# A transformer block with attention and a mixture of experts: the shared tiles leave PSUM by ScalarE, their sums move into the expert cycles, and all engines get a new order between the batches and the experts

## The reference

```python
h = layernorm(x) * (1 + ca) + sa                      # per batch
w = exp(tanh((h @ W + b) @ h.T * lw)); w = w * off_diag
x = x + ga * ((w / (sum(w) + 1e-7)) @ h)
h = layernorm(x) * (1 + cb) + sb
logits = h @ Wg                                       # 8 experts, the best 2 are taken
sparse = sum over the 2 chosen of softmax weight * (relu(h @ W1[e] + b1[e]) @ W2[e] + b2[e])
shared = relu(h @ Ws1 + bs1) @ Ws2 + bs2              # every token
out = x + gb * (sparse + shared)
```

## Time and profile before

| | |
|---|---|
| runs | 664.46, 659.73, 660.33 us; median 660.33 |
| profiled execution | span 665.5 us from the first to the last instruction; no time of its own is given beside the span |
| TensorE matmul busy | 618.6 us, 93% |
| VectorE busy | 457.9 us, 69% |
| ScalarE busy | 397.5 us, 60% |
| GpSimd busy | 343.3 us, 52% |
| mean granted TensorE clock | 0.982 |
| indirect DMAs on GpSimd | L576 x64 (of one source) 1008 ns each; L780 x138 1032 ns each |

### The profile page before, as it was taken

The page is one execution under the profiler, slowest core; times in us unless marked ns, Lnnn a source line. Parts: engine busy times, 40 slices in busy tenths (PEclk is TensorE's granted clock), DMA queues, the critical chain, the costliest instruction groups (busy, mean ns, idle before and its releaser), DMA issues.

```text
span 665.5 us, 13395 instructions
## 1 busy us (share of the span) xinstructions
PE 618.6 (93%) x4311; PEld 560.6 (84%) x4311; DVE 457.9 (69%) x1415; ACT 397.5 (60%) x635; POOL 343.3 (52%) x341
## 2 busy tenths in 40 slices
PE   3898999999999998977898999999999999999995
PEld 3587988898889886866798999998989898898995
DVE  7889797989898969766666564544444454452698
ACT  3587887877878756524346556565555646463541
POOL 4541706757575765657460465655565656465100
PEclk9899999999999999887999999999999999999998
DMA  8030000111111111111165466656666665521692
GB/s 299 27 158 1 1 1 17 37 34 33 34 33 38 33 42 33 37 39 43 49 196 200 129 197 190 181 172 193 195 188 182 187 182 178 175 65 30 268 386 113
DMA packets 29884, 76.44 MB, mean 115 GB/s; under 512 B 7126, under 2 KB 11374, under 8 KB 29712
## 3 DMA queue, kind: packets, MB, share of 16 engines
q1 hardware_dynamic: 20480, 58.49, 27.2%
q0 software_dynamic: 8640, 16.93, 7.5%
q10 hardware_dynamic: 720, 0.47, 0.2%
HBM read 53.53 MB, written 23.24 MB: 115 GB/s over the span
## 4 chain that ended last, share of the span: by engine, by line
PE 33%; DVE 8%; issue 5%; another core or an unknown queue 2%; DMA 2%; POOL 2%; ACT 1%; SPq 0%; POOLq 0%; ACTq 0%; DVEq 0%
PE value L1940 12%; PE score L1733 5%; PE misc L1940 5%; PE score L1731 5%; PE score L1732 4%; PE value L1991 2%; POOL rows_x L576 2%; DVE h_hi L1271 1%; DMA h_t<-rows_z 1%; ACT work L967 1%; DVE tile_y L1560 1%; PE misc L1772 1%; DVE tile_y L1552 0%; DMA lw<-rows_x 0%
## 5 line engine op out<-in xcount | busy, mean ns | idle before, releaser
L780 POOL DMA_INDIRECT rows_z<-tile_y,tags x138 | 142.5, 1032 | 118.8 <-issue 37.5
L1731 PE MATMUL score<-h_hi,h_lo 128*128 128x512 f32 (+1 forms) x252 | 94.9, 376 | 3.9 <-DVE rows_all L1177 3.8
L1759 PE MATMUL value<-w_ring,work 128*128 128x129 f32 x768 | 93.8, 279 | 1.6 <-ACT work L840 1.0
L1759 PEld LDWEIGHTS value<-w_ring,work 128*128 128x128 f32 x768 | 91.2, 194 | 4.1 <-issue 1.6
L967 ACT ACTIVATE work<-score,w_ring 128x512 f32<-128x512 f32 (+1 forms) x96 | 53.2, 616 | 61.7 <-PE score L1733 44.5
L1733 PE MATMUL score<-h_hi,h_lo 128*128 128x512 f32 (+1 forms) x252 | 89.4, 355 | 0.0
L1732 PE MATMUL score<-h_hi,h_lo 128*128 128x512 f32 (+1 forms) x252 | 88.9, 353 | 0.0
L576 POOL DMA_INDIRECT rows_x<-work,slot x64 | 64.5, 1008 | 45.5 <-issue 16.3
L838 ACT ACTIVATE work<-work 128x1024 f32<-128x1024 f32 x64 | 67.2, 1050 | 27.2 <-DVE work L1168 22.1
L1168 DVE TENSOR_TENSOR work<-score,lw 128x1024 f32<-128x1024 f32 x64 | 76.6, 1216 | 2.7 <-PE score L1733 1.2
L967 ACT ACTIVATE work<-score,w_shared 128x512 f32<-128x512 f32 x64 | 39.9, 685 | 57.9 <-PE score L1733 45.6
(11 more groups left out here) (254 smaller groups left out, 1269.0 us busy)
## 6 DMA issues: line engine op xcount, KB each, us to landing
w_ring<-packs SPq DMA_DIRECT2D x24, 578.0 KB
rows_all<-packs SPq DMA_DIRECT2D x23, 578.0 KB
lw<-rows_x SPq DMA_DIRECT2D x24, 260.0 KB
res<-x SPq DMA_DIRECT2D x8, 512.0 KB, 6.3
h_t<-rows_z SPq DMA_DIRECT2D x3, 1024.0 KB, 11.0
mod<-mod_rows SPq DMA_DIRECT2D x1, 2560.0 KB, 10.1
rows_z<-tile_y,tags POOLq DMA_INDIRECT x142
rows_all<-rows_z SPq DMA_DIRECT2D x2, 1024.0 KB, 13.0
```

The costliest lines, as they stand in the source:

```text
L780: nc.gpsimd.indirect_dma_start(rows_z[:, :], bass.IndirectOffsetOnAxis(ap=tags[pos][:, k, 0:1].bitcast(I32), axis=0), tile_y[par][:, k, :] ...
L1731: nc.tensor.matmul(out, a_lo, b_hi, start=True, stop=False)
L1759: ins = nc.tensor.matmul(value[:, s // 3, c0:c0 + D + 1], prob[:, t % 4, s * P:(s + 1) * P], normal[b % 3][:, t, :], start=(t == 0 and s % ...
```

## The change

- **ScalarE takes the front shared tiles out of PSUM.** A new `evacuate_shared(n)` waits for `down_ready` n + 1 and copies the bank, without bias or gate, into the place in `h2_t` that held the tokens of tile n, and signals `y_evac`. The eight copies stand between the relus of the front tiles, the last behind `expert_x(0, 0)`.
- **VectorE adds them later.** `shared(n)` is gone. `add_shared_part(b, part)` does bias, gate and sum for a whole batch of 1024 tokens, one instruction a call; twelve calls for batches 0 to 3 stand in the six steps of expert cycles 1 and 2. These two cycles are written out on VectorE, and its loop begins at cycle 3. A wait for all eight copies stands ahead of cycle 0.
- **TensorE's order.** `shared_up(0)` and `shared_up(1)` come before the wait for `attend(7)`; then down 0, up 2, down 1, both transposes of batch 7, up 3, gate logits, down 2, ranks, up 4, total ranks, down 3. From `shared_up(5)` on nothing changes. Before, the order was up 0, down 0, up 1, up 2, transposes, gate logits, down 1, ranks, down 2, up 3, total ranks, up 4, down 3.
- **VectorE's order.** Both first splits come before `attend(7)`; `take_ranks(6)` and `assign(6)` come before `scale_attended(7)`; `moments_2(7)` comes right behind `add_attended(7)`; the other splits stand behind it.
- **ScalarE's order.** `split_x(3)` and `relu(2)` come before the staging of batch 7, `relu(3)` before `gap_exponent(7)`.
- **GpSimd's order.** `rstd_2(7)` comes after 7 sends instead of 9, and the three waits for `hidden_ready` among the last 29 sends are gone.

```diff
@@ -723,46 +723,11 @@
                     pool.wait_ge(*((last_second, 1) if b == B - 1 else (second_rows, b + 1)))
                 scatter(b, m)
 
-            send_next()
...
+            for _ in range(7):
+                send_next()
             rstd_2(B - 1)
-            send_next()
...
-            pool.wait_ge(hidden_ready, 5)
-            send_next()
...
-            pool.wait_ge(hidden_ready, 9)
-            send_next()
...
-            pool.wait_ge(hidden_ready, 12)
-            send_next()
...
+            for _ in range(29):
+                send_next()
 
 
             def send(i, pos, paced=True):
@@ -980,24 +945,36 @@
             act.wait_ge(score_ready, G * B)
             split_x(1, 1, shared_rows(1))
             gap_exponent(B - 2)
+            def evacuate_shared(n):
+
+                act.wait_ge(down_ready, n + 1)
+                nc.scalar.activation(shared_rows(n), yacc[n % 2], ACT.Copy).then_inc(y_evac, 1)
+
             act.wait_ge(value_step, G * B)
             relu(0, w_shared, 0)
             split_x(2, 0, shared_rows(2))
             relu(1, w_shared, 1)
+            split_x(3, 1, shared_rows(3))
+            evacuate_shared(0)
+            relu(2, w_shared, 0)
             stage_h2t(B - 1, 0)
             stage_h2t(B - 1, 1, xt_ps)
-            split_x(3, 1, shared_rows(3))
             split_x(4, 0, shared_rows(4))
-            relu(2, w_shared, 0)
+            evacuate_shared(1)
+            relu(3, w_shared, 1)
             gap_exponent(B - 1)
-            relu(3, w_shared, 1)
             split_x(5, 1, shared_rows(5))
+            evacuate_shared(2)
+            relu(4, w_shared, 0)
             split_x(6, 0, shared_rows(6))
-            relu(4, w_shared, 0)
+            evacuate_shared(3)
             relu(5, w_shared, 1)
             split_x(7, 1, shared_rows(7))
+            evacuate_shared(4)
             relu(6, w_shared, 0)
+            evacuate_shared(5)
             relu(7, w_shared, 1)
+            evacuate_shared(6)
             act.wait_ge(h2t_staged, 2 * B)
 
             def expert_w(i, pos):
@@ -1022,6 +999,7 @@
 
             expert_w(0, 0)
             expert_x(0, 0)
+            evacuate_shared(FRONT - 1)
             expert_w(0, 1)
             expert_x(0, 1)
             expert_relu(0, 0)
@@ -1420,16 +1398,20 @@
 
             batches(dve, batch)
 
-            def shared(n):
-                par, half = n % 2, n % 2
-                dve.wait_ge(down_ready, n + 1)
-                step = Chain(dve, y_step, 2 * n)
-                bias = w_shared[:, B2_AT:PACK].rearrange("p (o d) -> p o d", o=1).to_broadcast([P, K, D])
-                step(nc.vector.tensor_tensor(tile_y[par][:, :, :], yacc[par].rearrange("p (k d) -> p k d", k=K), bias, ALU.add))
-                gate = mod[:, n // 2:n // 2 + 1, 4, :].to_broadcast([P, K, D])
-                step(nc.vector.tensor_tensor(tile_y[par][:, :, :], tile_y[par][:, :, :], gate, ALU.mult))
-                r = res[:, (n // 2) * G + K * half:(n // 2) * G + K * half + K, :]
-                nc.vector.tensor_tensor(r, r, tile_y[par][:, :, :], ALU.add).then_inc(y_evac, 1)
+            shared_chain = Chain(dve, y_step, 0)
+
+            def add_shared_part(b, part):
+
+                y = h2_t[:, b * S:(b + 1) * S].rearrange("p (g d) -> p g d", d=D)
+                r = res[:, b * G:(b + 1) * G, :]
+                if part == 0:
+                    bias = w_shared[:, B2_AT:PACK].rearrange("p (o d) -> p o d", o=1).to_broadcast([P, G, D])
+                    shared_chain(nc.vector.tensor_tensor(y, y, bias, ALU.add))
+                elif part == 1:
+                    gate = mod[:, b:b + 1, 4, :].to_broadcast([P, G, D])
+                    shared_chain(nc.vector.tensor_tensor(y, y, gate, ALU.mult))
+                else:
+                    shared_chain(nc.vector.tensor_tensor(r, r, y, ALU.add))
 
             own, before_ = slice(E // 2, E // 2 + E), slice(E // 2 - 1, E // 2 + E - 1)
 
@@ -1493,37 +1475,30 @@
 
             count_chosen(B - 2, route_chain[B - 2])
             split_w(0, 0, w_shared)
+            split_x(0, 0, shared_rows(0))
+            split_x(1, 1, shared_rows(1))
             attend(B - 1)
-            split_x(0, 0, shared_rows(0))
+            take_ranks(B - 2)
+            assign(B - 2)
             scale_attended(B - 1)
-            take_ranks(B - 2)
             add_attended(B - 1)
-            assign(B - 2)
-            split_x(1, 1, shared_rows(1))
+            moments_2(B - 1)
             split_x(2, 0, shared_rows(2))
-            shared(0)
-            moments_2(B - 1)
+            split_x(3, 1, shared_rows(3))
             normalise_2(B - 1, last_xhat)
             last_rows()
+            split_x(4, 0, shared_rows(4))
             route_chain[B - 1] = choose(B - 1)
             count_chosen(B - 1, route_chain[B - 1])
             take_ranks(B - 1)
-            split_x(3, 1, shared_rows(3))
             assign(B - 1)
-            shared(1)
-            split_x(4, 0, shared_rows(4))
+            split_x(5, 1, shared_rows(5))
             total_counts()
             large_tiles()
-            split_x(5, 1, shared_rows(5))
-            shared(2)
+            split_x(6, 0, shared_rows(6))
             small_tiles()
             small_table()
-            split_x(6, 0, shared_rows(6))
-            shared(3)
             split_x(7, 1, shared_rows(7))
-            shared(4)
-            shared(5)
-            shared(6)
 
             def add_bias(b):
 
@@ -1569,16 +1544,20 @@
 
             expert_split(0, 0)
             expert_tags(0, 0)
-            shared(FRONT - 1)
             expert_split(0, 1)
             expert_tags(0, 1)
             expert_split(0, 2)
             expert_tags(0, 2)
+            dve.wait_ge(y_evac, FRONT)
             for pos in range(CYCLE):
                 expert(0, pos)
                 if 0 < pos <= B - FRONT // 2:
                     add_bias(FRONT // 2 - 1 + pos)
-            with dve.Fori(1, CYCLES - 1) as i:
+            for i in range(1, 3):
+                for pos in range(CYCLE):
+                    expert(i, pos)
+                    add_shared_part(*divmod(CYCLE * (i - 1) + pos, 3))
+            with dve.Fori(3, CYCLES - 1) as i:
                 for pos in range(CYCLE):
                     expert(i, pos)
             for pos in range(CYCLE - 4):
@@ -1959,21 +1938,21 @@
             values(B - 1, 1, G - 2)
             values(B - 1, 1, G - 1)
             ranks(B - 2)
+            shared_up(0)
+            shared_up(1)
             pe.wait_ge(value_used, B)
-            shared_up(0)
             shared_down(0)
-            shared_up(1)
             shared_up(2)
+            shared_down(1)
             pe.wait_ge(rank_used, B - 1)
             transpose_h2(B - 1, 0, misc, last_xhat)
             transpose_h2(B - 1, 1, xt_ps, last_xhat)
+            shared_up(3)
             gate_logits(B - 1)
-            shared_down(1)
+            shared_down(2)
             ranks(B - 1)
-            shared_down(2)
-            shared_up(3)
+            shared_up(4)
             total_ranks()
-            shared_up(4)
             shared_down(3)
             shared_up(5)
             shared_down(4)
```

More of the change, by code:

```diff
@@ L724, in send_next @@
                 scatter(b, m)
-            send_next()
-            send_next()
-            send_next()
-            send_next()
-            send_next()
[L731 to L734, removed]
-            rstd_2(B - 1)
[L736 to L741, removed]
-            pool.wait_ge(hidden_ready, 5)
[L743 to L752, removed]
-            pool.wait_ge(hidden_ready, 9)
[L754 to L757, removed]
-            pool.wait_ge(hidden_ready, 12)
[L759 to L765, removed]
+            for _ in range(7):
+                send_next()
+            rstd_2(B - 1)
+            for _ in range(29):
+                send_next()
             def send(i, pos, paced=True):
```

## The result

The changed kernel took 676.58 us (median of 4 runs, 675.69 to 681.02) against 660.03 us before, on the same chip: a ratio of 1.0249, 95% interval 1.0217 to 1.0281. The forecast was 652.4 us, in a range of 646.0 to 658.5.

The account below looks back on a forecast made before the run. Between 284.8 and 354.0 us, TensorE's own work and the chain to the first expert rows were taken to bind almost together. A gain of 8.4 us, less 0.5 for the cycles, gave 7.9 from 660.33: 652.4 us, range 646 to 658.5.

Parts of the forecast that it names:

- without the two paced waits ... 20.6: 335.0: GpSimd's sends of batch 7: without 3.7 us of waits, the last starts 20.6 us behind the slots, at 335.0.
- four ups, four downs: TensorE from batch 7's ranks at 311.4: with ranks and total ranks 26.2 us of work, free at 337.6.
- late wakes: Unexplained extra delays before batch 7's slots: 1.8 us at `attend(7)`, 3.7 us at `choose` and `count_chosen`; reckoned with and without.
- start of up 0 to slots of batch 7: Routing chain in the rewritten stretch: from up 0 at 285.2 to slots ready at 314.4, 29.2 us.
- slots to first rows: Sends, landing and load of batch 7's rows: from slots at 314.4 to rows at 340.5, 26.1 us.
- TensorE's wait for the rows: At the end of the stretch, the rows bind and TensorE idles for up to 2.9 us.
- twelve late adds: VectorE in cycles 1 and 2: adds of 1.22 us each, cost taken as 0.5 us, between 0 and 14.6.
- ScalarE's copies: Eight copies of 0.60 us between relus of the front tiles, 4.8 us together, claimed at no cost.
- The lead of the new order in the stretch: Gain up to the first expert rows, like against like 8 to 9 us, taken as 8.4.
- rival A: TensorE's wait for the rows halves the clock; `shared_down(7)` costs 2.0 us more; gain 5.9, 654.4 us; chance 0.14.
- C: Late adds in cycles 1 and 2 delay VectorE's splits by 14.6 us in all, 666.5 us; chance 0.05.
- B: Late wake at `attend(7)` makes up 2 wait 2.7 us, clock halves there and at the logits; 657.6 us; chance 0.16.

Follow-up runs that it names:

- Run 2: The kernel before with only the changed kernel's GpSimd stream (no waits, rstd_2 two sends earlier); 680.00 us, ratio 1.0190 to the kernel before.
- 3: The changed kernel with two GpSimd memsets as a gap behind every third to fifth send; 671.37 us, ratio 1.0045 to the kernel before.
- 4: The kernel of 3 with one more gap, ahead of the four left-over sends of batch 5; 666.90 us, ratio 0.9975 to the kernel before.
- 1: The changed kernel with the GpSimd stream of the kernel before, waits included; 674.35 us, ratio 1.0131 to the kernel before.
- 6: The kernel before with the GpSimd stream of 4, nothing else changed; 672.13 us, ratio 1.0068 to the kernel before.
- run 16: The changed kernel itself, unmodified, timed on a chip without stalls; 647.61 us, ratio 0.9949 to the kernel before.
- run 10: The kernel before with only ScalarE's copies and VectorE's late adds, all orders and waits as before; 650.96 us, ratio 1.0000 to the kernel before.
- run 17: The kernel of run 2, unchanged, timed on a chip without stalls; 650.79 us, ratio 0.9993 to the kernel before.
- 8: The kernel of 4 without the gap ahead of batch 7's first send and with the last 8 sends back to back; 654.17 us, ratio 1.0046 to the kernel before.
- 9: The changed kernel with gaps in the last 16 sends only; 649.95 us, ratio 0.9985 to the kernel before.
- 5: The kernel of 4 with one memset instead of two in the three gaps of the last 16 sends; 664.11 us, ratio 0.9953 to the kernel before.

## Why the prediction was wrong

The step that failed is the one that took the waits out as pure delay ("without the two paced waits ... 20.6: 335.0") and left every duration beside the sends as it was. The sends themselves held: from the slots to the last send the first comparison took 19.7 us. What did not hold is the other engines' work beside an unbroken run: the slots came 44.1 us behind the start of `shared_up(0)`, not 29.2, and TensorE's "four ups, four downs", ranks and total ranks took 39.7 us, not 26.2. Run 2 shows with GpSimd's stream alone that unbroken runs cost time on such a chip, runs 3 and 4 show it the other way round. The traces of the first comparison and of run 2 have the same stutter, but the changed kernel was not timed beside a paced twin on such a chip: that the first comparison's loss is the same effect rests on its trace and on runs 1, 2, 4 and 6.

The warning was in the rows of before. I called the extra 1.8 and 3.7 us "late wakes", said that the code explains neither, and let them stay as large in the new kernel or vanish. I did not look at what GpSimd did beside them. `attend(7)` started late beside the sixth of a row of sends, and `top_f`, a copy inside `choose` and `count_chosen`, was due 10.8 us after the start of a run of eleven that began at 304.52. The two waits of 1.87 and 2.42 us that I priced as pure delay kept the last run in pieces, and run 2 prices what happens without them.

Point by point, with run 16 for the chip without stalls, counted from the start of `shared_up(0)`:

| step | predicted | run 16 | first comparison |
|---|---|---|---|
| start of up 0 to slots of batch 7 | 29.2 us | 29.5 us | 44.1 us |
| slots to last send | 20.6 | 21.9 | 19.7 |
| ranks of batch 7 to TensorE free for the rows | 26.2 | 26.2 | 39.7 |
| slots to first rows | 26.1 | 27.2 | 36.7 |
| TensorE's wait for the rows | up to 2.9 | 4.15 | none |
| SyncE's pads | 9.4 | 8.7 | 16.15 |
| twelve late adds | 0.5 | none seen (200.00 of 200 us; run 10) | none seen |
| ScalarE's copies | 0 | none seen (run 10) | not separated |

So the new order was laid out right to within 1.4 us where the engines don't disturb each other. Even there the gain was 3.6 to 4.3 us, not 7.9. Two terms were mis-sized. The lead of the new order in the stretch is smaller than I had it: in run 17, with the old order, the rows come at 344.01, against 339.09 in run 16, so 4.9 us and not 8.4. The new order took the 1.4 us more of the table, and the old one 2.3 us less: 62.0 us from the ranks of batch 6 to the rows, where I had 64.3. And rival A's mechanism showed: behind its wait of 4.15 us TensorE's clock was 0.65 in the next 4 us,

```profile
339.00:343.00 4.00, 3.91 (x24) 3.94 (x25) 0.77 (x2) 0.60 (x1) 0.00 (x0) 0.65 0.92 279
```

and from the first rows to the end run 16 takes 305.4 us, run 17 with no wait 304.1: 1.3 us, where I had 2.0; run 17 also lacks the adds in its cycles, so the two are not separated here. By the Trainium skill, "TensorE: Matmul & The Clock Gate", section "HAM oscillation", a wait for a DMA can throttle the array; here the trace agrees. The wait of 3.01 us that I had set beside it was one for VectorE.

Of the rivals, C gave the sign but not the mechanism: the adds in cycles 1 and 2 stood on no path. B named a late wake at `attend(7)`; the wakes did multiply, but by run 2 it was the change itself that brought them.

**What stays open.** Whether the stalls belong to certain chips or to the hour: the first comparison and the first two groups had them, the last three groups did not, and the groups differ in both chip and time. And which part is shared between GpSimd's indirect DMAs and the other engines' instructions; no run tells whether rows, descriptors or something else counts, nor whether the engines' loading of their own instructions is what is held up. A gap on GpSimd ends the stall, so it is not the total of the sends. Experiments 8 and 9 could not place the harm among the three runs of sends.

## What to carry to other kernels

A wait that paces a queue may be there for the other engines: before taking it out, look for unexplained "remote" or "issue" idle time on them and lay it beside the queue that runs at that moment. If such idle time has no cause in the code, treat it as a term that the change can multiply, not as a constant. And time a close change on more than one chip: the same kernel was 2.5% slower in the first comparison and 0.5 to 0.6% faster on three chips.

## What the runs showed of the hardware that was not expected

- Indirect DMAs of 128 rows issued by GpSimd every 1.26 us without a break went with stalls of TensorE, VectorE, ScalarE and SyncE in the first comparison and in run 2. TensorE's began 9.4 us after the start of the run (changed kernel, last 16 sends) and lasted to its end, with the DMA engines 0.28 busy. At 1.54 us a send, in groups of four, none was seen beside the last sends; at 1.40 us there was a smaller stutter (runs 4 and 5).
- A stalled TensorE issued single matmuls at distances of about 0.7, 1.4, 2.1 and once 2.8 us.
- On three other chips the same runs of sends did nothing, and the kernel before took 651 us instead of 660 to 668. TensorE was busy for 200.00 us of the window from 400 to 600 us there, and for 194.75 to 197.50 us where the stalls occur.
